# Passage from the token chunks to the qkv steps: chunk 10's two products added by TensorE, chunk 11's products ahead of the statistics, qkv's low half behind chunk 1

## The reference, cut to what matters

```python
h = _L0_tok_ref(...)                        # a state-space filter: K[c,h,l] = 2 Re sum_n C[c,h,n] B[h,n] dA[h,n]**l
h = h + _L0_attn_ref(_layernorm(h), ...)    # inside: layer norm 1, qkv, elu(q)+1, elu(k)+1, linear attention, proj,
                                            # layer norm 2, fc1, gelu, fc2
h = h + _L0_ffn_ref(_layernorm(h), ...)     # a tree of gates over 256 leaves, an output product
```

## Time and profile before

| | us |
|---|---|
| median of 3 runs | 509.61 (508.94 to 510.22) |
| the profiled execution | 510.19 |
| its span | 508.4 |
| PE busy | 437.0 (86%) |
| DVE busy | 358.3 (70%) |
| ACT busy | 291.4 (57%) |
| POOL busy | 195.7 (38%) |

### The profile page before, as it was taken

One profiled execution on the slowest core, in us unless ns is written; L12 is line 12 of the kernel. 1 busy time (PEld: TensorE's weight loads), 2 busy tenths in 40 slices (PEclk: granted clock), 3 DMA queues, 4 the chain that ended last, 5 costly groups with the idle time before them and its releaser, 6 DMA issues.

```text
span 508.4 us, 11407 instructions
## 1 busy us (share of the span) xinstructions
PE 437.0 (86%) x3808; PEld 400.3 (79%) x3808; DVE 358.3 (70%) x867; ACT 291.4 (57%) x604; POOL 195.7 (38%) x187
## 2 busy tenths in 40 slices
PE   0048663999899999999999999999999999998974
PEld 0037663988788899888988988988988988998973
DVE  5998998995887676547476476476486586484774
ACT  3804553788876777566356457457448448446630
POOL 0496998761241210515406306306207207206020
PEclk9997997899999999999999999999999999999998
DMA  4532666344343101101002002002002001001011
GB/s 125 186 125 69 171 165 178 92 130 129 115 134 102 63 22 43 41 1 43 1 1 83 0 0 83 0 0 83 0 0 83 0 0 41 0 0 43 3 34 50
DMA packets 39871, 30.95 MB, mean 61 GB/s; under 512 B 19488, under 2 KB 35232, under 8 KB 39840
## 3 DMA queue, kind: packets, MB, share of 16 engines
q1 hardware_dynamic: 29280, 27.81, 18.0%
q10 hardware_dynamic: 10560, 2.75, 2.3%
HBM read 17.97 MB, written 12.58 MB: 60 GB/s over the span
## 4 chain that ended last, share of the span: by engine, by line
PE 71%; DVE 11%; issue 6%; ACT 4%; SPq 3%; DMA 2%; POOL 2%; DVEq 0%; ACTq 0%; POOLq 0%
PE PS L312 18%; PE PS L314 18%; PE PS L313 17%; PE PS L1476 5%; PE PS L1468 4%; PE PS L1586 3%; PE PS L1518 3%; DMA fc2raw<-in_fc2T 2%; DVE M L1048 2%; DVE Mb L1040 2%; DVE lTl L1211 1%; PE PS L1485 1%; DVE outb L1271 1%; PE PS L1538 1%; PE PS L1528 1%
## 5 line engine op out<-in xcount | busy, mean ns | idle before, releaser
L1240 DVE TENSOR_TENSOR gl<-PS,gh 128x512 fp32r<-128x512 f32 x56 | 38.7, 691 | 62.1 <-ACT gh L809 34.4
L806 ACT ACTIVATE PS<-PS,fc1bias 128x512 f32<-128x512 f32 x56 | 36.7, 655 | 75.2 <-PE PS L314 74.3
L312 PE MATMUL PS<-fc2h,gh 128*128 128x256 f32 x256 | 73.6, 288 | 2.9 <-DVE gl L1240 1.5
L538 POOL TENSOR_SCALAR pst<-mv 128x4 f32<-128x4 f32 x15 | 4.2, 282 | 185.1 <-DVE pst L1224 185.1
L314 PE MATMUL PS<-fc2l,gh 128*128 128x256 f32 x256 | 71.4, 279 | 0.0
L313 PE MATMUL PS<-fc2h,gl 128*128 128x256 f32 x256 | 71.3, 279 | 0.0
L312 PE MATMUL PS<-x2Th,fc1h 128*128 (+2 forms) x144 | 54.5, 379 | 0.0
L312 PEld LDWEIGHTS PS<-fc2h,gh 128*128 128x128 f32 x256 | 48.0, 188 | 7.0 <-DVE pst L1224 1.6
L313 PE MATMUL PS<-x2Th,fc1l 128*128 (+2 forms) x144 | 53.0, 368 | 0.0
L314 PE MATMUL PS<-x2Tl,fc1h 128*128 (+2 forms) x144 | 52.9, 367 | 0.0
L313 PEld LDWEIGHTS PS<-fc2h,gl 128*128 128x128 f32 x256 | 48.2, 188 | 1.0
(11 more groups left out here) (233 smaller groups left out, 1408.4 us busy)
## 6 DMA issues: line engine op xcount, KB each, us to landing
h<-h_scratch SPq DMA_DIRECT2D x16, 256.0 KB, 3.5
q_scratch<-qe SPq DMA_DIRECT2D x16, 256.0 KB, 2.3
qf<-q_scratch SPq DMA_DIRECT2D x16, 256.0 KB, 2.9
out_tokens<-outb SPq DMA_DIRECT2D x16, 256.0 KB, 2.2
h_scratch<-tokev ACTq DMA_DIRECT2D x10, 256.0 KB, 2.9
craw<-in_c_ri SPq DMA_DIRECT2D x16, 128.0 KB, 2.4
craw<-in_c_ri SPq DMA_DIRECT2D x32, 64.0 KB, 2.4
h_scratch<-tokev SPq DMA_DIRECT2D x6, 256.0 KB, 2.9
```

What stands on the lines that cost most here:

```text
L312: pe.matmul(dst, ah, bh, start=start, stop=False, **kw)
L806: act.activation(bank(j % 2), bank(j % 2), ACT.Gelu, bias=fc1bias[:, j:j + 1]).then_inc(gact, 1)
L1240: dve.tensor_tensor(gl[:, j % 2, :], bank(j % 2), gh[:, j % 2, :].bitcast(F32), ALU.subtract).then_inc(gldone, 1)
```

## The change

1. Chunk 10's two products are no longer added by VectorE. The first is written straight into M, the second into a new SBUF tile `Mc`, and TensorE multiplies both (`unsummed_tokens`): after each matmul of M a second one of `Mc`, 56 columns wide, into the shifted columns of the same region.
2. Chunk 11's products stand ahead of the first statistics, its sum behind them.
3. qkv's low half, the bias sum and the two copies of ones go from the place behind chunk 10 and the first statistics to the place behind chunk 1. Chunks 0 and 1 come out of VectorE's loop for it.
4. In step 0, `norm1_apply(1)` and `norm1_apply(2)` go between chunk 12's products and its sum. `k_elu(0, 0)` goes ahead of `y_low(1)`. TensorE transposes step 1's tokens between the two kv products of step 0, and ScalarE's `y_high(1)` goes between its two `kv_parts`. Every later `norm1_stats` in these steps comes one step later; that of step 7 goes to step 4 of the next loop.
5. GpSimd's `rotate(12)` waits for the two normalized tiles of step 0, and no longer for the two small operations behind them; `rotate(13)` waits for those of step 2. ScalarE makes the tables of chunk 11 before it evicts chunk 9, and those of chunk 12 behind the eviction of chunk 10.

The core of the diff (waits whose number alone changes, and the counting function `products_done`, which gives 3 a chunk and one less from chunk 10 on, are left out):

```diff
+            def unsummed_products(n):
+                dve.wait_ge(xyld, CREDIT + n + 1)
+                dve.wait_ge(tokmm, CREDIT + n - 1)
+                product(n, 7, 0, M[:, n % 2, :, :, 1:NE])
+                product(n, 7, 1, Mc[:, :, :, :])
...
             dve.wait_ge(pool_set, POOL_TABLES)
-            with dve.Fori(0, PAIRS // 2) as it:
+            for n in range(2):
+                products(n, 7 - n)
+                product_sums(n, n)
+            dve.wait_ge(act_set, 1)
+            tt(qkvl[:, :, :], qkvraw[:, :, :], qkvh[:, :, :].bitcast(F32), ALU.subtract)
...
+            tt(fc1bias[:, :], fc1bias[:, :], b1add[:, :], ALU.add)
+            dve.wait_ge(pool_set, POOL_TABLES + 6)
...
+            link(dve.tensor_copy(vt[:, :, :, P], one.to_broadcast([P, 2, KD])))
+            link(dve.tensor_copy(vt0[:, :, :, P], one.to_broadcast([P, B, KD])))
+            with dve.Fori(1, PAIRS // 2) as it:
...
-            products(SINGLE, 7)
-            product_sums(SINGLE, SINGLE % 2)
+            unsummed_products(SINGLE)
+            single_product(SINGLE + 1, 0)
+            single_product(SINGLE + 1, 1)
             norm1_stats(0)
...
+            single_sums(SINGLE + 1)
             norm1_apply(0)
             norm1_stats(1)
-            products(SINGLE + 1, 7)
-            product_sums(SINGLE + 1, 1)
             norm1_stats(2)
             y_low(0)
...
+            def unsummed_tokens(n):
...
+                    for x, w in enumerate((Wa, Wb)):
+                        c = w[:, n % 2, i, :, :].rearrange("p c d -> p (c d)")
+                        pe.matmul(dst, c, M[:, n % 2, i, :, :].rearrange("p a e -> p (a e)"), start=x == 0, stop=False,
+                                  skip_group_check=True)
+                        mm = pe.matmul(shifted, c, Mc[:, i, :, :], start=False, stop=x == 1, skip_group_check=True)
```

More of the change, by code:

```diff
@@ L44 @@
 SPREAD = STEPS - 5
-STATS = {5: (8,), 6: (9,), 7: (10, 11), 8: (12,), 9: (13,), 10: (14,), 11: (15,)}
+STATS = {4: (7,), 5: (8,), 6: (9,), 7: (10, 11), 8: (12,), 9: (13,), 10: (14,), 11: (15,)}
 LEVELS = 8
@@ L157, in vit_tower @@
         qraw_at = cursor[0]
+        cursor[0] = tables_at + size([P, 2, KD, HT])
+        Mc = sb("Mc", [P, CH, NA, EX])
+        assert cursor[0] <= qraw_at
+        cursor[0] = qraw_at
         qe = sb("qe", [P, 2, KD, HT])
@@ L291, in sums_bank, with products_done @@
             return 7 if c % 2 and c not in (5, 7) else 0
+        def products_done(n):
+            return 3 * (n + 1) - (n >= SINGLE)
         def sums_before(c):
@@ L513, in _ @@
             scales(0)
-            pool.wait_ge(xh1, CREDIT + 4)
+            pool.wait_ge(xh1, CREDIT + 2)
             rotate(FIRST // 2, 0)
@@ L517, in _ @@
             scales(2)
+            pool.wait_ge(xh1, CREDIT + 4 * 2 + 2)
             for n in range(FIRST, CHUNKS - 1):
@@ L760, in _ @@
             operands(SINGLE)
+            tables(SINGLE + 1)
             closed(SINGLE // 2 - 1, 1)
             operands(SINGLE + 1)
-            tables(SINGLE + 1)
-            for n in range(SINGLE + 1, CHUNKS):
+            token_row(SINGLE)
+            tables(SINGLE + 2)
+            operands(SINGLE + 2)
+            y_high(0)
+            for n in range(FIRST, CHUNKS):
                 s = n - FIRST
                 token_row(n - 1)
-                y_high(s + 1)
-                if s >= 0:
-                    q_parts(s)
+                if s > 0:
+                    y_high(s + 1)
+                q_parts(s)
                 if n + 1 < CHUNKS:
@@ L772, in _ @@
                     tables(n + 1)
-                if s >= 0:
-                    kv_parts(s, 0)
-                    kv_parts(s, 1)
+                kv_parts(s, 0)
+                if s == 0:
+                    y_high(s + 1)
+                kv_parts(s, 1)
             token_row(CHUNKS - 1)
@@ L1029, in _, with product @@
             assert count[0] == DVE_U, count[0]
+            Ma = PS[:, 2:4, :].rearrange("p b x -> p (b x)")[:, 0:CH * NA * EX].rearrange(
+                "p (h a e) -> p h a e", h=CH, a=NA)
+            def product(n, b, r, to):
+                xy = PS[:, b, 0:D].rearrange("p (h x a) -> p h x a", h=CH, x=2)
+                x = xy[:, :, r, :].unsqueeze(3).to_broadcast([P, CH, NA, EX])
+                w = (Er, Ei)[r][:, bass.ds(n * CH, CH), :].unsqueeze(2).to_broadcast([P, CH, NA, EX])
+                dve.tensor_tensor(to, x, w, ALU.mult).then_inc(vdone, 1)
             def products(n, b):
@@ L1033, in products @@
                 dve.wait_ge(vdone, CREDIT + 3 * n)
[L1034 to L1040, removed]
+                product(n, b, 0, Ma)
+                product(n, b, 1, Mb[:, :, :, :])
             def product_sums(n, par):
@@ L1118, in kv_mask @@
                                   mask8.unsqueeze(1).to_broadcast([P, KD, HPB]), ALU.mult).then_inc(kvdone, 1)
-            products(SINGLE, 7)
-            product_sums(SINGLE, SINGLE % 2)
+            unsummed_products(SINGLE)
+            single_product(SINGLE + 1, 0)
+            single_product(SINGLE + 1, 1)
             norm1_stats(0)
[L1123 to L1131, removed]
+            single_sums(SINGLE + 1)
             norm1_apply(0)
             norm1_stats(1)
-            products(SINGLE + 1, 7)
-            product_sums(SINGLE + 1, 1)
             norm1_stats(2)
             y_low(0)
-            norm1_stats(3)
-            norm1_apply(1)
             for n in range(FIRST, CHUNKS):
                 s = n - FIRST
-                products(n, 7)
-                product_sums(n, n % 2)
-                y_low(s + 1)
-                q_elu(s)
[L1146 to L1149, removed]
+                single_product(n, 0)
+                single_product(n, 1)
+                if s == 0:
+                    norm1_apply(1)
+                    norm1_apply(2)
+                single_sums(n)
+                if s > 0:
+                    y_low(s + 1)
+                q_elu(s)
+                if s > 0:
+                    norm1_apply(s + 2)
+                else:
+                    k_elu(s, 0)
+                    y_low(s + 1)
+                norm1_stats(s + 3)
+                if s > 0:
+                    k_elu(s, 0)
                 k_elu(s, 1)
@@ L1162, in step @@
                     kv_mask(image(s - 1, 1))
-                if s > 5:
+                if s != 5:
                     for x in STATS.get(s, ()):
@@ L1462, in tokens @@
                 pe.wait_ge(m0done, CREDIT + n + 1)
-                pe.wait_ge(vdone, CREDIT + 3 * (n + 1))
+                pe.wait_ge(vdone, CREDIT + (products_done(n) if b is None else 3 * (n + 1)))
+                b = b or 0
                 for i in range(CH):
@@ L1469, in tokens @@
                                        M[:, par, i, :, :].rearrange("p a e -> p (a e)"), start=x == 0, stop=x == 1)
+                mm.then_inc(tokmm, 1)
+            def unsummed_tokens(n):
+                pe.wait_ge(wdone, CREDIT + 2 * (n + 1))
+                pe.wait_ge(c0done, CREDIT + n + 1)
+                pe.wait_ge(m0done, CREDIT + n + 1)
+                pe.wait_ge(vdone, CREDIT + products_done(n))
+                pe.wait_ge(tokout, CREDIT + n - 1)
+                for i in range(CH):
+                    rows = slice(64 * (i % 2), 64 * (i % 2) + 64)
+                    dst = PS[rows, 0, (i // 2) * SH:(i // 2 + 1) * SH]
+                    shifted = dst.rearrange("p (a e) -> p a e", a=NA)[:, :, 1:NE]
+                    for x, w in enumerate((Wa, Wb)):
[3 more added lines that the diff above has]
+                        mm = pe.matmul(shifted, c, Mc[:, i, :, :], start=False, stop=x == 1, skip_group_check=True)
                 mm.then_inc(tokmm, 1)
@@ L1547, in _ @@
             pe.wait_ge(staged, 2)
-            for n in range(SINGLE, CHUNKS):
+            unsummed_tokens(SINGLE)
+            y_transposes(0)
+            pe.wait_ge(tokout, CREDIT + SINGLE + 1)
+            tokens(SINGLE + 1, 1, None)
+            pe.wait_ge(dve_set, DVE_ALL)
+            for n in range(FIRST, CHUNKS):
                 s = n - FIRST
+                if s > 0:
+                    y_transposes(s + 1)
+                q_products(s)
+                kv_products(s, 0)
                 if s == 0:
-                    pe.wait_ge(dve_set, DVE_ALL)
-                if s + 1 >= 0:
                     y_transposes(s + 1)
[L1554 to L1559, removed]
+                kv_products(s, 1)
+                pe.wait_ge(tokout, CREDIT + n)
+                tokens(n, n % 2, None)
             def step(s):
```

20 lines of the change are left out of this document (15 added, 5 removed).

## The result

| | before | after |
|---|---|---|
| median | 509.58 (508.88 to 510.22, 6 runs) | 512.66 (511.85 to 513.62, 6 runs) |
| the profiled execution | 510.19 | 512.29 |
| its span | 508.4 | 510.5 |

The ratio is 1.0055, 95% interval 1.0043 to 1.0067: 2.2 to 3.4 us slower. 512.5 was forecast.

A forecast was written before the change was run, and what follows sets the result against it. VectorE's queue was taken to set the time until the steps begin. Terms: -0.56 + 6.63 (early) - 5.05 (passage) + 1.85 (elu against rotate) = +2.9 us, on 509.61 giving 512.5; range 506.4 to 514.4.

The forecast's parts named there:

- Early loss: Behind chunk 1, small VectorE instructions each wait for a GpSimd rotation half; everything from chunk 3 on 6.1 us later.
- Passage: From chunk 10 to chunk 12's tokens, the rewriting wins back 5.05 of the 6.1 us lost early.
- the tokens of the first statistics: Ahead of step 0's statistics: their tokens landed long before, so the old DMA wait of 0.37 us is gone.
- Elus: Steps 0 and 1: q_elu and k_elu wait for halves of GpSimd's rotations; 1.85 us lost.
- nothing is lost from step 2 on: In the later steps VectorE's period is 6.89 us and TensorE's about the same; nothing is won or lost.
- No collisions: Rival: VectorE's instructions slip in beside GpSimd's; early loss 1.9 us, -3.1 in all, 506.5 us; chance 0.19.
- the rival in which only the elus wait: Rival: the early instructions slip in, q_elu and k_elu don't; -1.3 us, 508.3 us; chance 0.08.
- GpSimd holds on: Rival: GpSimd lets nobody in between its halves; chunk 2 at 54.45, 1.6 us more, 514.1 us; chance 0.13.
- The clock: Rival: TensorE's clock falls before the first transposes; 0.5 us on them, 1.7 on chunk 11's tokens; 513.6 us; chance 0.06.
- Tokens of chunk 10 dearer than 4.1: Rival: TensorE's matmuls for chunk 10 exceed 4.1 us through shifted columns; costs nothing up to 6.5 us; no chance given.

The follow-up runs named there:

- rotate2_waits: The changed kernel, with GpSimd's rotation of chunk 2's matrices waiting until VectorE's four once-only instructions are done; 508.57 us, ratio 0.9981 to the kernel before.
- chunk10_summed: The changed kernel, but VectorE adds chunk 10's two products and TensorE multiplies one tile for it; 513.76 us, ratio 1.0069 to the kernel before.
- elu_first: The changed kernel, with GpSimd's rotations of chunks 13, 14, 15 waiting for VectorE's k_elu(0, 0), q_elu(1), q_elu(2); 515.01 us, ratio 1.0100 to the kernel before.
- all_late: The changed kernel, with all four once-only instructions behind chunk 11's sum, ahead of step 0's xh; 508.10 us, ratio 0.9951 to the kernel before.
- before_moved: The kernel before, with only the four once-only instructions moved behind chunk 1; 515.11 us, ratio 1.0094 to the kernel before.

## Why the prediction was right

The kernel came out slower by the mechanism forecast. Step by step, in the profiled execution:

- **Early loss.** Chunk 2 at 52.8 forecast, 52.54 measured; the bias sum and the copies were blocked one for one. That 6.1 reach chunk 10 was 0.5 too much: it starts 5.61 later (79.31 for 73.70 in the earlier trace rows). Of the difference 0.26 was there at chunk 2, the rest went on the way.
- **Passage.** From chunk 10 to the first transposes 8.75 forecast, 8.41 measured (79.31 to 87.72): the wait for ScalarE ahead of chunk 11 was 0.45 and not 0.7, and step 0's power took 1.03 without qkvl beside it, where 1.19 was reckoned. One step was wrong: the tokens of the first statistics had not landed long before. They come later as the chunks do, and VectorE still stood 0.17 for the DMA at 84.11. Chunk 12's tokens began at 96.51 for the 97.4 forecast, so the passage won back 5.45 of 5.61, not 5.05 of 6.1.
- **Elus.** q_elu(0) took 1.19: it waited for Wa's end (97.03) and ended at 97.47. Wb then took 2.06, ending 1.47 behind q_elu, and k_elu(0, 0) took 1.73 and ended at 99.12, just behind Wb (98.94). From chunk 12's tokens to the transposes of step 2 there are 3.35 us, 3.6 forecast and 2.06 before. With what step 1's q_elu (1.26) adds until T(5), the term of 1.85 measures 1.75: 1.91 at T(5) less 0.16 at chunk 12's tokens. Its parts came out otherwise: 1.3 up to T(3) for 1.55, and 0.4 from there to T(5) for 0.3, since q_elu(2) was held too (0.96 for 0.68). That nothing is lost from step 2 on did not hold: the steps from T(3) took 7.03 and 7.04 for 6.83 and 6.82.
- **The sum.** 6.07 - 5.05 + 1.85 = +2.9 forecast; on TensorE it is 5.61 - 5.45 + 1.75 = +1.9, and the profiled executions are 2.1 apart. The medians, 3.1 apart, lie nearer to the forecast than its terms deserve: 512.5 for 512.66 is in part luck, and the profiled execution, forecast at 513.1, took 512.29. The 1 us between medians and profiled executions lies in these two executions: before's was 0.6 above its median, after's 0.4 below. The clock in the last steps makes such differences elsewhere, but both have 1.00 in 490 to 495 us, so the cause stays open.
- **Rivals.** No collisions: refuted by five durations (1.34, 1.50, 1.45, 1.19, 1.73). With the early collisions alone taken away (rotate2_waits) the time is 508.57, where the rival in which only the elus wait had 508.3; no run is without all of them. GpSimd holds on: refuted, each waiting instruction got in behind one half, though the next was queued. The clock: not in this kernel (0.66), but in chunk10_summed. Tokens of chunk 10 dearer than 4.1: they were, 81.64 to 86.49, 4.85 us, and hidden, as said.

The Trainium skill ("SBUF — State Buffer", Who interferes with whom) names as contenders the VectorE operations with two SBUF inputs, and copies and tensor_scalar in a two-port mode, and says that one with at most one SBUF input outside these modes does not contend. The traces agree on both sides of the rotation: elus, copies, xh and mr were blocked (1.73, 1.50, 2.08, 1.45 us); y_low and the sums, with a PSUM operand, kept 0.68 and 1.09, and the statistics 0.74. Whether the copies and xh ran in such a mode no trace shows. By that rule xh and mr could have been counted before elu_first. The page puts no GpSimd instruction that reads SBUF apart from the others; here the power, which reads two SBUF tiles, let even a sum of two SBUF tiles pass (0.16 us), and the measurement decides.

## What to carry to other kernels

A tiny instruction of VectorE on SBUF tiles cost a whole half of a GpSimd rotation wherever halves were queued: put once-only work where VectorE waits anyway, and price it by its neighbour on GpSimd and not by its size. Look at that neighbour's kind too: the rotation blocked, the small power did not. Beside a long GpSimd instruction let VectorE do what ran there unslowed in a trace. Delaying GpSimd paid where VectorE's next instructions could not be blocked (rotate2_waits, 4.1 us); in the steps it moved the collision to whatever VectorE did next. Cut a change of two parts into both halves: here 4.8 us lost early hid about 2 won in the passage.

## What the runs showed of the hardware that was not expected

- GpSimd's power of four elements took 1.03 us and blocked nobody: three small ones ran in 0.16 to 0.20 beside it, and qkvl, which began at 81.66 within it (81.00 to 82.03), took its 1.76. The other way round, with qkvl running first, it took 2.41.
- Idle time of TensorE can cost twice: chunk10_summed has less work for it, and its next transposes ran at half clock behind a wait of 3.46 us. After, with 32 more matmuls ahead of a wait of 1.23, they ran at the full clock. Behind 3.16 (all_late) and 3.27 (before_moved) the transposes still took 0.66, but four matmuls of the tokens after them took 0.52 and 0.48 for 0.34.
- The granted clock fell in the early wait too: chunk 2's tokens began at half clock in after, behind 7.6 us of idling (0.48 us for each four matmuls, 0.34 later). VectorE didn't wait for them: from chunk 2 to chunk 10 it took 26.77 us, 3.35 a chunk.

```profile
55.81 0.49 PE L1516 MATMUL PS<-M,Wa 128*64 128x64 f32 x4 [7.60 <-DVE M L1065]
...
59.68 0.34 PE L1516 MATMUL PS<-M,Wa 128*64 128x64 f32 x4
```
